# A two-layer decoder in one program: SyncE's waits for stores put behind the stage barrier, GpSimd's drain left out in two kinds of stage, and another list schedule for the token stages

## What is computed

```python
x = _layernorm(x + _L0_attn_ref(x, ...))         # 16 heads of 16, ALiBi, half forward, half backward
x = _layernorm(x + _L0_xattn_ref(x, ctx_768, ...))
x = _layernorm(x + _L0_ffn_ref(x, ...))          # 8 experts, top 2, gated GELU, F = 704
x = _layernorm(x + _L1_attn_ref(x, ...))         # full attention
x = _layernorm(x + _L1_xattn_ref(x, ctx_768, ...))
x = _layernorm(x + _L1_ffn_ref(x, ...))          # RMS norm, causal attention over a latent,
                                                 # RMS norm, 8 experts, top 2, SiLU, F = 512
```

## Time and profile before

| | us |
|---|---|
| median of 3 runs | 2250.22 |
| lowest, highest | 2247.93, 2252.23 |
| the profiled execution | 2248.09 |
| its span | 2246.3 |
| TensorE busy in the span | 1953.8 |
| VectorE busy | 1293.8 |
| ScalarE busy | 994.6 |
| GpSimd busy | 491.3 |

### The profile page before, as it was taken

How to read it: one execution, slowest core, us unless ns; L and a number is a source line. 1 busy time by engine, 2 the same in 40 slices (tenths; PEclk the granted TensorE clock), 3 DMA queues, 4 the chain that set the end, 5 groups by cost and what they waited for, 6 DMA issues and landing times.

```text
span 2246.3 us, 32863 instructions
## 1 busy us (share of the span) xinstructions
PE 1953.8 (87%) x10990; PEld 1007.3 (45%) x10991; DVE 1293.8 (58%) x2318; ACT 994.6 (44%) x1919; POOL 491.3 (22%) x801
## 2 busy tenths in 40 slices
PE   8799999688499999948999999978887999967992
PEld 4344445334466666623222222254443444455661
DVE  3578874786522222256788888456576878562115
ACT  3156665476111111122666666734532666622331
POOL 3311102421132222112200000033151101043440
PEclk9699999799699999978899999988997999978996
DMA  8433313321810000036111130053135333061123
GB/s 232 122 61 60 48 18 72 86 45 52 315 47 30 31 30 30 26 117 142 30 29 29 30 49 9 1 142 59 38 73 109 53 53 58 2 188 45 63 65 122
DMA packets 111607, 157.90 MB, mean 70 GB/s; under 512 B 31543, under 2 KB 88695, under 8 KB 108535
## 3 DMA queue, kind: packets, MB, share of 16 engines
q1 hardware_dynamic: 103986, 135.75, 26.4%
q0 software_dynamic: 7488, 20.46, 2.8%
HBM read 110.44 MB, written 44.72 MB: 69 GB/s over the span
## 4 chain that ended last, share of the span: by engine, by line
PE 65%; DVE 10%; issue 9%; POOL 4%; DMA 4%; SPq 3%; ACT 3%; POOLq 1%; DVEq 0%; ACTq 0%
PE psum L1513 11%; PE psum L1471 11%; PE psum L2129 11%; PE psum L1495 9%; PE psum L2148 7%; PE psum L1026 3%; DVE arena L1587 3%; PE psum L995 3%; PE psum L2139 2%; DMA q_halves<-arena 1%; PE psum L1498 1%; PE psum L1528 1%; POOLq L2376 1%; ACT arena L1554 1%; DVE arena L1081 1%
## 5 line engine op out<-in xcount | busy, mean ns | idle before, releaser
L1554 ACT ACTIVATE arena<-psum 128x512 f32<-128x512 f32 (+1 forms) x1120 | 573.7, 589 | 367.7 <-PE psum L1495 183.2
L1587 DVE TENSOR_REDUCE arena<-psum 128x1 f32<-128x1024 f32 (+3 forms) x352 | 400.1, 1172 | 93.3 <-PE psum L1471 63.5
L1471 PE MATMUL psum<-arena 96*128 96x512 bf16 (+7 forms) x1280 | 366.8, 370 | 35.1 <-DVE arena L1630 17.0
L1495 PE MATMUL psum<-arena 99*128 99x512 bf16 (+7 forms) x1280 | 365.8, 353 | 11.6 <-ACT arena L1554 6.7
L1513 PE MATMUL psum<-arena 128*32 128x512 f32 (+3 forms) x2560 | 281.4, 538 | 1.0 <-ACT arena L1554 1.0
L1573 DVE CUSTOM_DVE_ANT_0 arena<-psum,arena 128x640 bf16<-128x640 f32 (+3 forms) x256 | 250.1, 1021 | 55.8 <-PE psum L1471 54.5
L2129 PE MATMUL psum<-arena 128*128 x780 | 269.8, 493 | 1.7 <-ACT arena L2183 1.1
L1471 PEld LDWEIGHTS psum<-arena 96*128 96x128 bf16 (+1 forms) x1280 | 100.6, 100 | 278.3 <-issue 82.7
L1495 PEld LDWEIGHTS psum<-arena 99*128 99x128 bf16 (+1 forms) x1280 | 123.8, 98 | 184.8 <-ACT arena L1554 76.2
L2233 DVE COPY arena<-psum 128x640 f32<-128x640 f32 (+1 forms) x78 | 59.2, 758 | 253.3 <-PE psum L2139 253.3
L2148 PE MATMUL psum<-arena 128*128 (+1 forms) x780 | 189.0, 384 | 2.1 <-DVE arena L2236 1.2
(11 more groups left out here) (205 smaller groups left out, 2391.4 us busy)
## 6 DMA issues: line engine op xcount, KB each, us to landing
arena<-k_parts SPq DMA_DIRECT2D x144, 128.0 KB
q_halves<-arena SPq DMA_DIRECT2D x80, 192.0 KB, 3.1
arena<-q_halves SPq DMA_DIRECT2D x40, 384.0 KB, 4.8
arena<-q_halves SPq DMA_DIRECT2D x40, 256.0 KB, 5.3
k_parts<-arena SPq DMA_DIRECT2D x48, 192.0 KB, 3.3
arena<-in_L_ffn_w SPq DMA_DIRECT2D x9, 1024.0 KB, 11.8
arena<-y_rows SPq DMA_DIRECT2D x32, 256.0 KB, 4.3
arena<-in_L_ffn_w SPq DMA_DIRECT2D x8, 704.0 KB, 9.1
```

Source lines behind the costliest of these rows:

```text
L1471: last = nc.tensor.matmul(dst[:, base + lo:base + hi], q[0:rows, qh, h, qb % 4 * P:qb % 4 * P + P], k[0:rows, h, key0 + lo:key0 + hi], sta ...
L1495: last = nc.tensor.matmul(b[:, at0:at0 + width], kk[0:rows, h, kb * P:kb * P + P], q[0:rows, qh, h, c0:c1], start=True, stop=diag is None)
L1554: nc.scalar.activation(probs[k % 4][:, heads[0]:heads[-1] + 1, c0:c1], bank[st_bank[no % 3]][:, 0:len(heads) * width].rearrange("p (h q) - ...
L1587: nc.vector.tensor_reduce(dst, src, AX.X, ALU.max).then_inc(t("taken"), 1)
```

## The change

It has five parts.

1. **Behind the barrier.** A stage may now have a program `sp_behind`, which SP runs after it has added its count to `stage_done`. For token stages it holds the waits for the landing of the last stores, for the context's stores in `t0`, and, in `t2` and `t6`, the last of the eight calls of `between_sp` (the weights of expert 7 and with them the down weights). The semaphores of these stores have a name of their own for each stage, so that GpSimd doesn't clear them. Also, `store_rows` of a pair is now issued ahead of `between_sp` of that pair, not behind it.
2. **No drain.** In the routing and the expert stages GpSimd adds its count without a drain. In `ex0` it first waits for its own additions of the bias.
3. **t3 and t7.** In `t3` the loads of the weights after next are issued behind the fourth `load` of rows. ACT starts both stages with a square root of one column, which loads its table.
4. **The list schedule.** The tail of a step now counts the later steps of its own kind too (`path_lengths`), 150 further orders with shifted ranks are drawn, and the one whose last step (SP's left out) ends first by the planner's estimates is kept. In `t3` and `t7` the first four loads have an estimate of 5.0 in place of 3.5.
5. Semaphore names only: `out_sem` in place of `t("scr...")`.

```diff
-def list_order(tasks):
-    (tail of a key: its us + lag + the largest tail among its users)
+def path_lengths(tasks):
+    users, kinds, tail = {key: [] for key in tasks}, {}, {}
+    for key, (eng, us, lag, needs) in tasks.items():
+        for x in needs:
+            if x in tasks:
+                users[x].append((key, tasks[x][2]))
+        same = kinds.setdefault(key[0], [])
+        if same:
+            users[key[0], same[-1]].append((key, 0.0))
+        same.append(key[1])
...
+def list_order(tasks):
+    draw = np.random.RandomState(1)
+    tail = path_lengths(tasks)
+    kinds = sorted({kind for kind, n in tasks})
+    rank, best = tail, order_by(tasks, tail)
+    for turn in range(150):
+        shift = dict(zip(kinds, draw.uniform(-8.0, 8.0, len(kinds))))
+        other = {key: (rank if turn % 2 else tail)[key] + shift[key[0]] + draw.uniform(-0.5, 0.5) for key in tasks}
+        found = order_by(tasks, other)
+        if found[1] < best[1]:
+            rank, best = other, found
+    return best
...
-                        task("SP", "load", p, 1.0, 3.5, ("add", p - 4))
+                        task("SP", "load", p, 1.0, 5.0 if p < 4 else 3.5, ("add", p - 4))
...
             def sp_prog(sp):
-                if wn is not None and has_in and next_weights:
+                if wn is not None and source == "proj" and next_weights:
                     load_weights(sp, wn + 1)
...
                         load_rows(sp, n)
+                        if n == 3 and wn is not None and next_weights:
+                            load_weights(sp, wn + 1)
                     elif kind == "keep":
-                        between_sp(sp, n)
                         store_rows(sp, n)
+                        if n + 1 < n_pairs:
+                            between_sp(sp, n)
...
-                for place in range(NPLACE if nqk else 0):
-                    sp.wait_ge(t(f"scr{place}"), stored(nqk))
                 if context:
                     context.store_values(sp)
+
+            def sp_stored(sp):
+                for place in range(NPLACE if nqk else 0):
+                    sp.wait_ge(out_sem(place), stored(nqk))
+                if context:
+                    context.stored(sp)
+                if between_sp:
+                    between_sp(sp, n_pairs - 1)
...
             def act_prog(act):
+                if source == "comb":
+                    nc.scalar.activation(idle_col, eps_col[:, 0:1], ACT.Sqrt).then_inc(t("table"), 1)
...
-            progs = {"sp": sp_prog, "dve": dve_prog, "pool": pool_prog, "act": act_prog}
+            progs = {"sp": sp_prog, "dve": dve_prog, "pool": pool_prog, "act": act_prog, "sp_behind": sp_stored}
...
                 if n + 1 < len(stages):
-                    eng.drain().then_inc(stage_done, 1)
+                    if key == progs.get("undrained"):
+                        eng.sem_inc(stage_done, 1)
+                    else:
+                        eng.drain().then_inc(stage_done, 1)
+                if f"{key}_behind" in progs:
+                    progs[f"{key}_behind"](eng)
```

67 lines of the change are left out of this document (38 added, 29 removed).

## The result

The kernel after takes 2220.36 us (median of four runs, 2214.51 to 2225.86) beside 2249.07 for before (four runs, 2246.19 to 2252.23): a ratio of 0.9872, 95% interval 0.9838 to 0.9905. It was run once more beside later experiments: 2218.33 us, 0.9853 (0.9836 to 0.9869). So it is faster by some 30 us; 50 were forecast, and 2220 lies 1 us above the range. The profiled execution took 2224.16 us, its span is 2222.4. The chain over the whole span can't be set beside the earlier trace rows, since it loses its thread at the barrier that GpSimd opens without a drain; what follows is read stage by stage.

What follows compares the result with a forecast made beforehand. Outside the unchanged attention and expert stages, it took barrier waits and the token stages' order of steps as the bound. Terms (a) to (h) sum to 50.0 us off 2248.1, giving 2198.1, median forecast 2199 us, range 2187 to 2219.

Steps and rivals of the forecast that it cites:

- (a): End of t0: the barrier needs only the issue of the vx store, not its landing; 5.4 us gain.
- (b): Ends of t1, t3, t4, t5: last store's landing off the barrier, 2.4 us each, less 0.5 for xa0 and xa1; 8.6 us.
- (c): Ends of ex0 and ex1: without GpSimd's 7.49 us drain the scatter's landing comes last; 4.4 us each, 8.8 together.
- (e): rt1: TensorE's next start needs the second fetch's issue and the first's landing, not the drain; 1.4 us (0.9 to 2.1).
- (d): Start of t3: SP issues rows ahead of weights; 1.9 us gain, nothing from the early table load in ACT.
- (h): New orders: t3 4.5, t5 8, t1 and t4 2 each, t0 a loss of 2; together 14.5 us.
- (f): End of t6: the four down weights move behind the barrier; 4.5 us gain.
- (g): t2 to ex0: barrier and drain give 7.1 us, but later weights delay TensorE's start in ex0; 4.9 us gain (0 to 7.1).
- Rival 1: The new orders give nothing: 2213 us, or 2222 with (c) at its lower bound; chance 0.16.
- rival 3: Slower: new orders feed TensorE in smaller pieces, keeping its clock low longer; above 2250 us, up to 2310; chance 0.02.
- rival 4: Scatters land as late as the drain ends, and the first fetch too, so (c) and (e) vanish: 2209 us; chance 0.09.
- the last sentence of the prediction: Sign of error: an engine starts early, then waits as long behind SP's wait, or t3's and t5's ends don't follow their fronts.

Runs made afterwards that it cites:

- late_context: Kernel after, but SP waits for the context's stores in at0, behind the second group's loads, not at the end of t0: 2220.33 us, 0.9877 of before.
- late_vx: Kernel after, but vx is stored in at0, behind the second group's loads and first row maxima, not in t0: 2211.34 us, 0.9828 of before.
- maxima_bias: maxima_first, but in self-attention stages GpSimd adds the bias behind the split of the second row maxima, not ahead of it: 2208.35 us, 0.9815 of before.
- maxima_first: Kernel after, but in self-attention stages SP issues the first row maxima ahead of the second group's loads: 2219.61 us, 0.9861 of before.
- undrained_only: Kernel before, but GpSimd signals without a drain in rt0, rt1, ex0 and ex1 (in ex0 with its bias wait): 2241.13 us, 0.9943 of before.
- early_weights: Kernel after, but SP issues expert 0's up weights at t2's start, expert n + 1's behind pair n's store: 2216.10 us, 0.9866 of before.
- t3_undrained: Kernel after, but in t3 GpSimd waits for the last of its own thirds and signals without a drain too: 2219.99 us, 0.9838 of before.
- mended: Kernel after with t3_undrained, late_context, early_weights and split_wait together, and the old order in t0 alone: 2203.15 us, 0.9800 of before.
- split_wait: Kernel after, but in ex0 TensorE waits for up weights before its first transposes, for down weights only before their first product: 2213.23 us, 0.9863 of before.

## Why the prediction was wrong

(a) `t0`, 5.4 us forecast: **the gain is there, and the next stage pays more than it.** `at0` now begins 1.1 us after VectorE's last step in `t0`, before 6.6. The sentence that failed is "VectorE works on it for longer than 5 us, so nobody waits for them at once". The step named what is queued behind SP's wait (the ones, the second group, the first row maxima), and then asked only whether the engines had other work for those 5 us. It didn't ask when each of them is wanted, or what is queued behind them in turn. The row maxima are ready to be sent 11 us after the start and wanted by TensorE some 3 us later, and they land behind the second group's loads, which start 6.5 us late because vx is in front. `at0` pays 7.3 us for 5.4. Moving the wait for vx alone gives back 3.0 of them (late_context), sending vx later 6.2 (late_vx), and the order of what follows gives back all (maxima_bias). A second limit lies close behind the first: the weights that are queued last are wanted by GpSimd for a bias that stands in front of the second row maxima. In after it isn't yet the one that binds, since the split waits 5.41 us for VectorE when the addition is done:

```profile
112.57 7.88 POOL L1393 TENSOR_TENSOR arena<-arena 128x1024 f32<-128x1024 f32 x4 [14.13 <-DMA arena<-in_L_xattn_bq]
125.85 0.28 POOL L1646 CAST arena<-arena 32x128 bf16<-32x128 f32 x1 [5.41 <-DVE arena L1638]
```

It takes over as soon as the first row maxima come early (maxima_first).

(b) `t1`, `t3`, `t4`, `t5`, 8.6 us: mis-sized. From the last compute to the next stage `t1`, `t4` and `t5` went from 5.5, 5.2 and 4.2 us to 3.8, 3.8 and 2.4, so 1.3 to 1.8 each and not 2.4: compute now ends earlier against SP's issues. The half microsecond set aside for `xa0` was 2.8 by the one profile of before and 2.0 by the mean of the three with its code, and `mla`, for which nothing was, lost 3.5, all but 0.1 of them by the first row maxima behind the second group's loads, as in (a). TensorE's wait in `mla` of after:

```profile
1705.13 0.59 PE L1539 MATMUL psum<-arena 99*128 99x512 bf16 x1 [2.15 <-DMA arena<-arena]
```

Behind `t3` nothing was gained, but 2.3 us lost (3.1 us from the last compute to the next stage before, 5.4 after), by (c).

(c), (e) the drains, 10.2 us: right where they were removed. `ex1` to `t7` gained 4.3 us (4.4 forecast); `ex0` 5.0 in undrained_only (4.4); `rt1` 1.2 (1.4). The rival that a scatter lands only when the drain ends falls: the last scatter was issued at 968.24, and SP, which waits for its landing, issues loads at 970.76. What no step of the prediction had is that the drain's cost moves to the next drain, 4.5 us on the path at the end of `t3`. The prediction took the 7.49 us as the price of an instruction; it is a price of what was issued before it. "No drain" was costed by the rows of the place from which it was taken, and the next place of the same instruction, was not looked at.

(d) and (h) `t3`: together 6.4 us. From the last compute of `ex0` to the last of `t3` before took 85.0 us and after 72.1, 12.9 less, where (c), (d) and (h) asked for 10.8. Only the first transposes came less early than said (3.7, not 5.5 us), since the second add waits for rows.

(f) `t6`: 4.5 forecast, 4.6 measured.

(g) `t2` to `ex0`, 4.9 us forecast, 1.8 lost: the step that failed is a reading. "The queue runs full until 608.3" was taken for the landing of the last weights. It was that of the last but one; the last landed at 611.5, as the issue's own row says (600.8 + 10.7). With 611.5 + 3.7 = 615.2 the forecast would have been 1.7 us. Of the rest, 1.6 us are that the first store, and with it the queue, comes 10.05 us after the start of `t2` and not 8.5, and some 1.3 are what remains; that the fetches and the loads for `t3`, which used to come later, share the engines with the down weights would explain it, but wasn't tried. The price of the missing early load, 3.7 us, was right within some 0.2 us (3.7 and 3.9 in early_weights). Nor would the 358 GB/s of the Trainium skill ("DMA: Bandwidth & Descriptors", "Where 436 GB/s comes from") have saved the step: by it that load costs 4.0 us (an estimate), and the windows of `t2` at the end of this text show 405 GB/s, against it once more.

(h) Orders: 14.5 us forecast, 13.5 measured alone. `t5` gave 10.1 (8 forecast). `t0` cost 3.5 to 4.3 us in place of 2. Before and after wait for the same store, the new order at

```profile
55.79 0.69 ACT L975 ACTIVATE arena<-psum,arena 128x512 bf16<-128x512 f32 x1 [13.21 <-DMA q_halves<-arena]
```

and two of the context's steps of the same kind (line 1326, at 56.4 and 59.8) stand behind that `first` in ScalarE's list. In before two of them ran at 41.5 and 42.4, ahead of a wait of 10.44 us for that store. So more of the context is left for the time behind the wait. Windows of 47 to 57 and 57 to 67 us, after, then before (first number behind the length: TensorE busy):

```profile
47.00:57.00 10.00, 8.50 (x34) 3.70 (x32) 0.43 (x1) 1.21 (x3) 0.00 (x0) 1.00 1.01 219
57.00:67.00 10.00, 5.38 (x21) 2.68 (x22) 6.36 (x21) 5.15 (x10) 5.78 (x6) 0.69 0.45 121
```

```profile
47.00:57.00 10.00, 10.00 (x33) 4.45 (x31) 1.02 (x2) 1.73 (x3) 0.00 (x0) 1.00 0.93 235
57.00:67.00 10.00, 6.81 (x35) 3.77 (x34) 7.13 (x21) 4.84 (x10) 6.04 (x6) 0.83 0.66 180
```

TensorE is busy for 2.9 us less there. The planner has 3 us for the landing of a store; these four landed 8.4 to 9.9 us after their issue. That this is the whole of the cost in `t0` isn't shown.

Of the rivals none came true. Rival 1 with (c) at its lower bound names 2222, and both its halves are refuted: the orders gave 13.5 us, and the drains came off. That the time lies near 2222 is no support for it. Against rival 3 the granted clock rose, from 0.83 to 0.88 in `t3` and from 0.88 to 0.98 in `t5`; rival 4 falls with the landing under (c). The cause was spread over places in which something that a barrier had hidden came out from behind it, and only the last sentence of the prediction had named that: an engine that starts a stage early and then waits as long for a load behind SP's wait. It had no chance and no price of its own.

What stays open: why `xa0` differs by up to 6.5 us between profiles (144.5 to 151.0 with the same code), and what of its mean loss of 2.8 us is the second group (VectorE's 13th instruction comes 11.9 to 12.9 us after the first, 10.1 before; but in `xa1` it comes 12 to 13 us after it too, 10.1 before, and that stage is no longer than it was). A split of the store semaphores by group, which would let SP load it earlier, wasn't tried.

## What to carry to other kernels

A barrier hides whatever runs while all wait. Before counting its removal as a gain, put the transfers in flight at that moment and the next stage's own loads into one queue, with the time at which each is wanted, down to the last one and to every engine: what is wanted first must not stand last. When an expensive waiting instruction is removed, ask whether its price belongs to it or to what was issued before; if to the latter, look at the next instruction of its kind, and leave the price where an engine has slack. And take a landing from the row of the DMA itself, not from the moment at which the engines' busy share falls.

## What the runs showed of the hardware that was not expected

- A drain of GpSimd behind the scatters of `ex0` took 6.9 to 7.8 us however much ordinary work lay in between: 7.49 us right behind the last one (before), 7.64 us 70 us after it (after), 6.90 us 460 us after it (t3_undrained). With another drain between the scatters and it (before) it took 1.4 and 0.5 us at the ends of the same two stages, `t3` and `at1`. Behind the two fetches of `rt0` or `rt1` alone (before) it took 4.1 us.
- The time to land of a small DMA was set by the queue in front of it: the three row maxima (4 KB each) took 1.7 us with idle engines (maxima_first), 2.5 in before, and 9.5 right behind the second group's loads (after). The first fetch of rows took 6.1 us behind the down weights (mended), the third and fourth, later in `ex0`, 3.6 and 2.8.
- TensorE's granted clock falls to its lower level (0.50, 1.2 GHz) in `t2` at one of two moments. 24 to 28 us into the stage, in after and in split_wait, TensorE being busy without a break in both, it is still 1.00 in the first and has fallen in the second (0.65 over the window):

```profile
582.40:586.40 4.00, 4.00 (x39) 4.00 (x38) 2.22 (x10) 1.09 (x2) 1.65 (x4) 1.00 1.04 405
```

```profile
578.00:582.00 4.00, 4.00 (x27) 4.00 (x26) 2.27 (x10) 1.09 (x2) 1.78 (x4) 0.65 1.04 405
```

  With the same order of steps, `t2`'s compute is 34.0 us long in the one and 36.8 in the other. The 16 profiles with after's order of compute steps in `t2` are of one length or the other (34 or 37 us), eight and eight. So equal kernels differ by 2.8 us in this stage alone, which is a part of why single runs of after lie between 2214 and 2226 us, and why experiments of 4 us had to be read from stages and not from the total.
